# V pieces on other banks and spread over the leading maxima, third parts of batch 1 made by Pool, late weights loaded behind group 0, layer b's V in quarters

## The reference, cut to what matters

```python
x = x + attn_a(layernorm(x), Wq, bq, Wk, bk, Wv, bv, Wo, bo)   # 32 heads of 8, softmax over 1024 keys
x = x + ffn(layernorm(x), w_gate, w_up, w_down)                # silu(x Wg) * (x Wu), 2:4 sparsified, Wd
x = x + attn_b(layernorm(x), wq, wk, wv, wo)                   # 32 q heads, 8 kv heads, a banded mask
x = x + ffn(layernorm(x), w_gate, w_up, w_down)                # the same ffn and weights
```

## Time and profile before

| what | value |
|---|---|
| three executions | 1762.63, 1758.98, 1763.02 us (median 1762.63) |
| the profiled execution | 1761.46 us |
| its span, first to last instruction | 1759.7 us |
| mean granted TensorE clock | 0.977 of full speed |
| PE busy | 1675.1 us (95%) |
| DVE busy | 1494.2 us (85%) |
| ACT busy | 1272.6 us (72%) |
| POOL busy | 251.5 us (14%) |
| HBM read, written | 71.96 MB, 40.63 MB |

### The profile page before, as it was taken

One profiled execution on the slowest core, in us unless ns is written; L12 is line 12 of the kernel. 1 busy time (PEld: TensorE's weight loads), 2 busy tenths in 40 slices (PEclk: granted clock), 3 DMA queues, 4 the chain that ended last, 5 costly groups with the idle time before them and its releaser, 6 DMA issues.

```text
span 1759.7 us, 39225 instructions
## 1 busy us (share of the span) xinstructions
PE 1675.1 (95%) x13872; PEld 666.1 (38%) x13872; DVE 1494.2 (85%) x2158; ACT 1272.6 (72%) x2424; POOL 251.5 (14%) x609
## 2 busy tenths in 40 slices
PE   6889999999899999999997999999998999999999
PEld 3322222222222223777653222222222222247777
DVE  5989999999899993676677999999998999926655
ACT  3269999999799999333222999999997999973221
POOL 1220000000000000000001322333322233310000
PEclk9879999999999999999997999999999999999999
DMA  6853443333443311100304322223322222121000
GB/s 176 261 139 63 85 81 59 65 60 62 77 84 71 60 38 62 60 1 0 110 14 131 61 49 54 48 53 67 64 53 49 48 54 48 29 69 51 13 12 24
DMA packets 72124, 114.67 MB, mean 65 GB/s; under 512 B 12464, under 2 KB 27824, under 8 KB 71984
## 3 DMA queue, kind: packets, MB, share of 16 engines
q1 hardware_dynamic: 71984, 112.63, 28.2%
HBM read 71.96 MB, written 40.63 MB: 64 GB/s over the span
## 4 chain that ended last, share of the span: by engine, by line
PE 60%; DVE 27%; issue 7%; DMA 3%; ACT 2%; DVEq 1%; SPq 0%; POOL 0%; POOLq 0%; ACTq 0%
DVE mneg L1136 17%; PE psum L667 17%; PE psum L730 13%; PE psum L649 11%; DVE xn L1142 8%; PE psum L622 7%; PE psum L750 6%; PE psum L587 2%; DMA max_rows<-mT 2%; PE psum L710 2%; PE psum L606 1%; DVE mneg L1142 1%; ACT area L911 1%; PE psum L569 1%; DMA area<-max_rows 1%
## 5 line engine op out<-in xcount | busy, mean ns | idle before, releaser
L911 ACT ACTIVATE area<-psum 128x512 f32<-128x512 f32 x2048 | 1097.0, 601 | 98.7 <-PE psum L649 79.2
L667 PE MATMUL psum<-area 128*32 128x256 f32 x8192 | 645.2, 393 | 0.7 <-POOL area L1377 0.4
L649 PE MATMUL psum<-area 51*128 51x512 bf16 x2048 | 627.5, 388 | 19.1 <-DMA area<-max_rows 16.6
L1142 DVE CUSTOM_DVE_ANT_0 xn<-psum,band 128x1024 f32<-128x1024 f32 x512 | 595.6, 1221 | 28.6 <-PE psum L622 21.9
L1136 DVE TENSOR_REDUCE mneg<-psum 128x1 f32<-128x1024 f32 x512 | 588.0, 1214 | 25.2 <-PE psum L622 20.8
L667 PEld LDWEIGHTS psum<-area 128*32 128x32 f32 x8192 | 169.2, 108 | 379.0 <-issue 265.1
L649 PEld LDWEIGHTS psum<-area 51*128 51x128 bf16 x2048 | 138.6, 94 | 452.8 <-ACT area L911 381.4
L622 PE MATMUL psum<-area 48*128 48x512 bf16 x1024 | 293.8, 392 | 15.7 <-DVE mneg L1136 15.3
L622 PE MATMUL psum<-k_max_b,area 48*128 48x512 bf16 x1024 | 285.2, 389 | 18.9 <-DVE mneg L1142 18.2
L954 ACT ACTIVATE area<-psum 128x512 f32<-128x512 f32 x64 | 38.2, 597 | 158.9 <-PE psum L730 158.8
L1358 POOL TENSOR_TENSOR mparts<-mneg,nought 128x16 bf16<-128x16 f32 x64 | 14.1, 220 | 771.8 <-DVE mneg L1136 549.4
(11 more groups left out here) (70 smaller groups left out, 826.9 us busy)
## 6 DMA issues: line engine op xcount, KB each, us to landing
ctx_rows<-area SPq DMA_DIRECT2D x64, 256.0 KB, 4.1
area<-q_stacks SPq DMA_DIRECT2D x32, 384.0 KB, 7.3
area<-k_stacks SPq DMA_DIRECT2D x64, 192.0 KB, 5.7
area<-q_stacks_b SPq DMA_DIRECT2D x32, 384.0 KB, 5.8
area<-q_stacks SPq DMA_DIRECT2D x32, 192.0 KB, 4.5
area<-q_stacks_b SPq DMA_DIRECT2D x32, 192.0 KB, 3.3
area<-ctx_rows SPq DMA_DIRECT2D x16, 256.0 KB, 4.5
area<-inv_rows SPq DMA_DIRECT2D x16, 256.0 KB, 5.4
```

Of the source, the lines that this page charges most:

```text
L649: pe.matmul(psum[:, S_BANKS[slot % len(S_BANKS)], :], k_st[lo:lo + ROWS + PARTS, buf, 0 if a else head // 2, kt * P:(kt + 1) * P], q_st[lo ...
L667: mm = pe.matmul(psum[head * VW:(head + 1) * VW, PV_BANK, cols], vaug[:, buf, kt, head, :], probs[:, u % PRING, head, cols], start=(kt == ...
L911: act.activation(probs[:, u % PRING, head, :], psum[:, S_BANKS[slot_of(u, head, ahead) % len(S_BANKS)], :], ACT.Exp, scale=SCALE).then_inc ...
L1142: dve.tensor_tensor_reduce(band_out[:, c % 2, :], slot, band[:, at:at + SEQ], 1.0, -3.0e38, ALU.add, ALU.max, mneg[:, qh, col:col + 1]).th ...
```

## The change

- The two early pieces of V go to banks 4 and 5 and no longer wait for all transposes to be copied; chunk 1, the first on banks 4 and 5, waits for their copies instead.
- The other six pieces of layer a stand at chunks 1, 5, 17, 19, 21, 23. The transposition at chunk 19 no longer waits for all V copies.
- `low` of batch 1 is Pool's in both layers; VectorE keeps those of batch 0. Pool's eight in layer a stand ahead of its first `extend_v` and `split_max`; in layer b two stand ahead of `split_max` and four behind it.
- `load_late_weights` stands behind group 0 on SP.
- Layer b's V of batch 1 is made in four quarters of four matmuls, at chunks 19, 21, 23, 24, and copied once, a chunk earlier than before.

```diff
-        V_BANKS = [[(6, 7), (6, 7)], [(4, 4), (7, 7)]]
+        def v_bank(a, b, v):
+
+            if a:
+                return 7 if b else 4
+            return 4 + v if b == 0 and v < V_EARLY else 6 + v % 2
...
-        V_CHUNKS = [(1, 3, 9, 11, 13, 15), (CPH + 9,)]
+        V_CHUNKS = [(1, 5, CPH + 1, CPH + 3, CPH + 5, CPH + 7), (CPH + 3, CPH + 5, CPH + 7, CPH + 8)]
+        V_TILES = BT // len(V_CHUNKS[1])
...
                     move_max(a, 0, 0, 0)
-                if a == 0:
-                    load_late_weights()
                 stored_all(a, BATCH)
                 group(a, 0, 0, first=True)
+                if a == 0:
+                    load_late_weights()
...
                 elif b == 0 and v == 0:
                     pe.wait_ge(w_loaded[0], 32)
+                elif b == 0 and v == V_EARLY:
                     pe.wait_ge(ln_evac, 8)
...
+                        if a:
+                            project_v(a, 1, 0, tiles=range(V_TILES * v, V_TILES * (v + 1)))
+                        else:
+                            project_v(a, *divmod(V_EARLY + v, VCH[0]))
+                    if a == 0 and c == 1:
+                        pe.wait_ge(v_done, V_EARLY)
                     if a == 0 and c == CPH + 3:
                         pe.wait_ge(rest_done, BATCH * PCH[a])
-                        pe.wait_ge(v_done, BATCH * VCH[a])
                         turn_max(a, 0, 0)
...
                 if i < PCH[a]:
                     rest(a, b, i)
-                if i:
+                if i and b == 0:
                     low(a, b, i - 1)
...
+            def low(a, b, i):
+
+                j, half = ORDER[a][i]
+                w, m, rows = QUARTERS[a][j]
+                n, s = PBASE[a] + b * PCH[a] + i, QBASE[a] + b * NQ[a] + j
+                pool.wait_ge(mid_done, n + 1)
+                pool.tensor_tensor(parts[SLOT[s]][0:rows, 2, half * BANK:(half + 1) * BANK],
+                                  resid[a][0:rows, n % 2, :],
+                                  parts[SLOT[s]][0:rows, 1, half * BANK:(half + 1) * BANK],
+                                  ALU.subtract).then_inc(lo_done, 1)
...
                 if a == 1:
+                    for i in range(HALF):
+                        low(a, 1, i)
                     split_max(a, 0, 0)
+                    for i in range(HALF, PCH[a]):
+                        low(a, 1, i)
+                if a == 0:
+                    for i in range(PCH[a]):
+                        low(a, 1, i)
                 extend_v(a, 0, 0)
```

More of the change, by code:

```diff
@@ L522, in _ @@
                     move_max(a, 0, 0, 0)
+                stored_all(a, BATCH)
+                group(a, 0, 0, first=True)
                 if a == 0:
                     load_late_weights()
-                stored_all(a, BATCH)
-                group(a, 0, 0, first=True)
                 with sp.Fori(0, GPB // 2) as i:
@@ L590, in project_half, with project_v @@
                 mm.then_inc(proj_ready, 1)
-            def project_v(a, b, v):
+            def project_v(a, b, v, tiles=None):
                 if a == 1:
@@ L602, in project_v @@
                     pe.wait_ge(v_done, n - 1)
-                for t in range(per):
+                for t in tiles or range(per):
                     tok = b * SEQ + (v * per + t) * P
                     for k in range(DK):
-                        mm = pe.matmul(psum[:, V_BANKS[a][b][v % 2], t * width:(t + 1) * width], xnT[:, k, tok:tok + P],
+                        mm = pe.matmul(psum[:, v_bank(a, b, v), t * width:(t + 1) * width], xnT[:, k, tok:tok + P],
                                        w_a[a][2][:, k, :], start=(k == 0), stop=(k == DK - 1))
-                mm.then_inc(v_ready, 1)
+                if not tiles or tiles[-1] == per - 1:
+                    mm.then_inc(v_ready, 1)
             def max_scores(a, g, buf, c):
@@ L772, in attend @@
                     if c in V_CHUNKS[a]:
-                        v = (0 if a else V_EARLY) + V_CHUNKS[a].index(c)
-                        project_v(a, 1 if a else v // VCH[0], v % VCH[a])
+                        v = V_CHUNKS[a].index(c)
+                        if a:
[4 more added lines that the diff above has]
+                        pe.wait_ge(v_done, V_EARLY)
                     if a == 0 and c == CPH + 3:
                         pe.wait_ge(rest_done, BATCH * PCH[a])
-                        pe.wait_ge(v_done, BATCH * VCH[a])
                         turn_max(a, 0, 0)
@@ L1077, in copy_v @@
                 dve.wait_ge(v_ready, VBASE[a] + b * VCH[a] + v + 1)
-                bank = psum[:, V_BANKS[a][b][v % 2], :]
+                bank = psum[:, v_bank(a, b, v), :]
                 if a == 0:
@@ L1243, in attend @@
                         split_step(a, 1, P_FIRST[a] + (c - P_CHUNKS[a][0]) // 2)
-                    if c - 1 in V_CHUNKS[a]:
-                        v = (0 if a else V_EARLY) + V_CHUNKS[a].index(c - 1)
-                        copy_v(a, 1 if a else v // VCH[0], v % VCH[a])
+                    if a and c - 1 == V_CHUNKS[a][-1]:
+                        copy_v(a, 1, 0)
+                    if a == 0 and c - 1 in V_CHUNKS[a]:
+                        copy_v(a, *divmod(V_EARLY + V_CHUNKS[a].index(c - 1), VCH[0]))
                 group(a, 0)
```

## The result

The change took 1754.76 us (median of eight runs, 1754.09 to 1757.80), the kernel before beside it 1760.28 us (eight runs, 1757.20 to 1763.02): a ratio of 0.9971, 95% interval 0.9960 to 0.9982. That is 5.5 us by the medians. The time lies inside the range, at its upper end, and the gain is less than half of the 15.0 us forecast. The three runs of before that stood ahead of the prediction had a median 2.4 us above that of these eight. The mean granted clock rose from 0.977 to 0.981.

What follows compares the result with a forecast made beforehand. VectorE's maxima pace layer a's middle, so gains come only at the edges: 10.8 (lead-in) + 6.1 - 5.3 (late weights) + 3.4 (layer b) = 15.0 us, from 1761.46 to 1746.5, plus 1.2 for the median: 1747.5 us, range 1738 to 1756.

Steps and rivals of the forecast that it cites:

- Other banks for the early pieces: Layer a's lead-in: the early V pieces' wait vanishes; chunk 0 comes at 39.3 instead of 43.52, 4.2 of 6.2 us kept.
- V pieces spread, third parts on Pool: Layer a's lead-in: chunk 6's maximum at 51.4, first score at 80.3 by the engines; with the queue, lead-in gain 10.8 us.
- Late weights behind group 0: Groups 0 and 1 of layer a: 6.1 us saved in group 0, 5.3 given back in group 1, bounds 0 and 7.
- The bound from above: Group 1's wait for its row of maxima: group 0's pattern moved by 42.8 with a context store more, a stall of 4.5.
- Layer b: Layer b's lead-in: V in quarters beside maxima brings the first score 3.4 us earlier, bounds 1.5 and 4.
- A: The forecast: the stall moves to group 1; 1747.5 us, own range 1743 to 1752, chance 0.50.
- B: Rival: the weights fit into the queue's idle 5.5 us and the slack, the stall is gone for good; 1742, chance 0.27.
- its sign: B's sign: the two stores of rows in groups 0 and 1 are 37 us apart.
- C: Rival: DMA holds layer a's first score, rows land at 84 or later, clock low at the start; 1751.5, chance 0.16.
- D: Rival: TensorE paces the lead-in to chunk 27 as before, little but the start's 4.2 us remains; 1758, chance 0.05.
- E: Rival: slower, Pool's third part is long and becomes the pace of batch 1; 1768, chance 0.02.

Runs made afterwards that it cites:

- The first experiment: The changed kernel with the row of maxima of the second half ahead of the next-but-one max stack's four loads in SP's queue: 1725.15 us, ratio 0.9802.

## Why the prediction was right and wrong, by its steps

**Other banks for the early pieces: right, with one thing missed.** 3.99 us ahead at the first leading maximum, 4.2 forecast, and the wait in front of it is for the DMA, as foretold. But it is 3.06 us, not 1.7, and the clock is at 0.66 in 40 to 45 behind it: the V piece at 39.85 takes 3.53 us where the earlier trace rows have 1.99. Before, the half clock (0.53 in 36 to 41) fell on the early pieces (6.17). The price of one wait was moved, not removed.

**V pieces spread, third parts on Pool: right in kind, 1.7 too large.** From the end of chunk 15 to the maximum of chunk 25 the working holds to 0.1: 68.23 to 82.08 on VectorE is 13.85, forecast 13.8. The error lies ahead of it.

```profile
53.02 1.23 DVE L1147 TENSOR_REDUCE mneg<-psum 128x1 f32<-128x1024 f32 x1 [0.40 <-PE psum L629]
54.16 0.74 DVE L1111 SCALAR_TENSOR_TENSOR area<-psum,bqk,area 128x512 f32<-128x512 f32 x1
54.81 0.68 DVE L1091 TENSOR_TENSOR vsb<-psum,bv_rows 128x512 f32<-128x512 f32 x1
...
67.09 4.61 DVE L1147 TENSOR_REDUCE mneg<-psum 128x1 f32<-128x1024 f32 x4
```
```profile
L1364 POOL TENSOR_TENSOR area<-area 128x512 bf16<-128x512 f32 x12 | 13.9, 1155 | 67.8 <-ACT area L907 67.8
```

Chunk 6's maximum starts at 53.02, not 51.4, about what the slow V piece lost (3.53 less 1.99); and I left out the copy of the piece at chunk 5, which stands behind chunk 6 for 0.60. The Pool part was priced at 1.10 and takes 1.155; gaps of 0.6 to 3.3 us lie between them on Pool, so they are never the pace. TensorE found the row there 0.27 us late: the DMA queue bound it, a little outside the 80.7 to 82.9 that the step gave, and the row landed 7.7 us after its store. A further 0.69 was lost between the first score and group 0's row. In both traces the granted clock is 0.50 from the first score on, before for some 10 us, after for some 11.7; that fits, but what held it down longer isn't shown.

**Late weights behind group 0: the wrong one of two bounds.** The 6.1 saved in group 0 were 6.05. The give-back was put at 5.3 and is 7.36: a wait of 4.83 and 2.5 for the clock (0.60 in 145 to 150). The step that failed is "9.2 us, of which about 7 fall in the queue's idle time before 140". I counted bytes (and 3.6 MB are 3.8 in the units of the profile's rates, so 9.4 us). The weights did move at such rates (383 to 414 GB/s in 122 to 128). But the loads of the stacks, which come behind the weights, keep all DMA engines busy (share 1.11) at 168 GB/s, less than half of the 403 that I had counted with. The bound from above, group 0's pattern moved by a group, was the right model (4.5 against 4.83), and the kernel with the weights back ahead of group 0 shows it: 10.84 us of landing with the weights in one place and 10.43 in the other. The Trainium skill (DMA: Bandwidth & Descriptors, Queues, rings and completion order) has each DMA engine take its descriptors in ring order; all the landings here agree with it, 1.37 us behind an empty queue and over 10 behind a full one.

**Layer b: the gain too small, its price not seen.** First score from the transposes: 19.14 us, before 25.57, so 6.4 gained, not 3.4. A quarter takes 1.10 us on TensorE where I allowed 1.5, and my sum for a rest, three maxima and a copy had 5.5 us where its own rates give 4.7. Another 0.9 was forecast by nothing: the projection half behind the transposes took 2.85 us in place of 3.78, as the granted clock rose earlier (0.74 in 930 to 932, before 0.50 from 934 to 938). These instructions are not edited, and they take 2.51 to 3.78 over the twelve traces, so I count it as luck. Then the step that the prediction did not have at all: group 0 of layer b has the same order in SP's queue as layer a's, and its row, now close behind the group's eight loads, four of them the ones for maxima, gave 3.79 back.

**The sentence that failed** is the one under the first heading: "Whatever is won there moves all that follows forward, since the groups behind wait for nothing but their own steps." Behind group 1 TensorE waits for a row at three more places: both inverted sums and group 0 of layer b. The one in layer a took 1.56 us of what had been won (0.21 of it in the wait itself), the one in group 0 of layer b 3.79, the last about 0.4. The trace of before had the warning: its scores wait 16.6 us for rows, of which the prediction has only the 3.70 of group 0, and 7.38 and 5.08 stand at the inverted sums. The first experiment shows what the sentence left out: with the row ahead of the loads 1.5 us of these waits are left, and the same change is worth 11 to 14 us. From 15.0: less 1.7 and 0.7 in the lead-in, less 2.1 in group 1, less 1.6 at layer a's inverted sums, plus 2.5 in layer b's lead-in, less 3.8 behind it, less 0.3 at the end, is 7.3.

The rivals: A's mechanism happened. B fell, the two stores in groups 0 and 1 being 37.0 us apart, which I had named as its sign, while group 2's came 44.3 behind. The sign was badly chosen: it measures what group 0 saves, and group 1's stall shows one spacing later. C happened in small: the row was 0.27 us late for the first score and the clock low at the start, but the row landed and the first score came (83.08) before the 84 that C named. The forecast of A, with a range of its own up to 1752, was too low for the reasons above. D and E did not happen.

## What to carry to other kernels

Before adding up what upstream edits save, list every place behind them where a small urgent transfer stands in a queue behind big ones that nobody wants yet; each such place can take back what comes to it early, as three of them did here, and one that already stalls can be seen in the trace before. Put the urgent transfer first: here one statement moved gave 21 us on the kernel before and 30 on the changed one, more than all five edits together, and only then were these worth 11 to 14. And let one part's value be measured with the urgent transfer already in front, since the same quarters of V, and the same Pool parts, were worth nothing without that edit and about 5 and 7 us with it.

## What the runs showed of the hardware

- The landing of a store of 48x128 goes with what stands ahead of it in the queue: 1.37 us behind nothing, 2.57 with loads issued 5.6 us earlier, 7.20 right behind eight loads, 10.43 and 10.84 behind weights and eight loads.
- The DMA engines' share says more than GB/s. Shares of 1.04 and 1.11 go with 413 GB/s in the lead-in of the change and with 168 under stack loads.
- A wait of 3 to 5 us on TensorE is followed by half clock: 0.66 in the 5 us behind one of 3.06, 0.60 behind one of 4.83. Behind the 2.82 in layer b it was 0.50. Such a wait cost 1.3 to 1.6 times itself (3.79 for 2.82; 7.36 for 4.83; 6.1 for 3.70).
- Pool's subtraction takes as long for 64 partitions as for 128 (1152 and 1155 ns), and where VectorE runs maxima back to back beside it they stay 1.13 us apart (four from 67.09 in 4.61 above, with Pool at a subtraction from 67.91 to 69.06).
